# Where ScalarE copies a score maximum: ahead of both score pairs, or between them

## The reference

```
q, k, v = heads(ln(x) @ wq), heads(ln(y) @ wk), heads(ln(y) @ wv)   # 16 heads of 32
a = softmax(q @ k.T / sqrt(32))     # over the keys: 512 in a1, 1024 in a2
if causal: a = a * (key > query)    # masked after the softmax
o = a @ v
x_out = x + o @ li1 + b1
return x_out + gelu(ln(x_out) @ li2 + b2) @ li3 + b3
```

## Time and profile before

| | |
|---|---|
| median of 3 runs | 1487.85 us (1482.93 to 1493.84) |
| the profiled execution's own time | 1473.39 us |
| its span, first to last instruction | 1471.6 us |
| PE busy | 1408.9 us, 96% |
| DVE busy | 860.0 us, 58% |
| ACT busy | 761.9 us, 52% |
| POOL busy | 583.0 us, 40% |
| a1's steps | from about 797 to 914 us of the span |
| a2's steps | from about 1034 to 1246 us |

### The profile page before, as it was taken

One profiled execution on the slowest core, in us unless ns is written; L12 is line 12 of the kernel. 1 busy time (PEld: TensorE's weight loads), 2 busy tenths in 40 slices (PEclk: granted clock), 3 DMA queues, 4 the chain that ended last, 5 costly groups with the idle time before them and its releaser, 6 DMA issues.

```text
span 1471.6 us, 24770 instructions
## 1 busy us (share of the span) xinstructions
PE 1408.9 (96%) x9882; PEld 804.9 (55%) x9902; DVE 860.0 (58%) x1768; ACT 761.9 (52%) x1161; POOL 583.0 (40%) x657
## 2 busy tenths in 40 slices
PE   8999999999999989999899999999999999999997
PEld 5677853333333257885643334743344444768996
DVE  3288647669999555136854784346788882323221
ACT  4644225666666646333255776332687886333331
POOL 3053134232424332621113665401688887406111
PEclk9999999999999999999999999997799999998999
DMA  7000000000120039774000001403000000652100
GB/s 228 1 1 1 1 12 1 12 9 19 44 41 19 3 123 317 231 254 43 2 22 1 2 1 59 129 0 136 1 1 2 2 2 30 252 199 89 55 10 10
DMA packets 75210, 86.96 MB, mean 59 GB/s; under 512 B 27161, under 2 KB 60917, under 8 KB 73942
## 3 DMA queue, kind: packets, MB, share of 16 engines
q1 hardware_dynamic: 72182, 79.10, 17.0%
q0 software_dynamic: 2912, 6.26, 1.2%
HBM read 64.25 MB, written 21.37 MB: 58 GB/s over the span
## 4 chain that ended last, share of the span: by engine, by line
PE 80%; DVE 11%; POOL 3%; issue 2%; ACT 2%; DMA 1%; SPq 0%; POOLq 0%; DVEq 0%; ACTq 0%
PE psum L1715 11%; PE psum L1734 9%; PE psum L1679 6%; PE psum L4126 5%; PE psum L736 4%; PE psum L3387 4%; PE psum L3378 4%; PE psum L1931 4%; PE psum L1757 3%; DVE a_nm L1844 3%; PE psum L4137 3%; PE psum L3356 2%; PE psum L724 2%; PE psum L751 2%; PE psum L1965 2%
## 5 line engine op out<-in xcount | busy, mean ns | idle before, releaser
L1844 DVE TENSOR_REDUCE a_nm<-psum 128x1 f32<-128x512 f32 x302 | 198.4, 681 | 90.7 <-PE psum L1679 86.0
L1844 DVE TENSOR_REDUCE xa_nm<-psum 128x1 f32<-128x512 f32 x256 | 161.8, 682 | 49.6 <-PE psum L1679 44.1
L1769 ACT ACTIVATE xn<-psum 128x1024 f32<-128x1024 f32 (+1 forms) x96 | 86.2, 949 | 51.0 <-PE psum L1715 51.0
L1769 ACT ACTIVATE a_w<-psum 128x1024 f32<-128x1024 f32 x86 | 83.4, 1021 | 20.5 <-PE psum L1715 19.7
L1769 ACT ACTIVATE xa_w<-psum 128x1024 f32<-128x1024 f32 (+2 forms) x96 | 79.7, 885 | 19.6 <-PE psum L1715 19.4
L1715 PE MATMUL psum<-a2qT,a2kT 32*128 32x512 f32 x512 | 87.2, 608 | 0.0
L1679 PE MATMUL psum<-a2kr,a2qr 32*128 32x512 bf16 x256 | 73.2, 410 | 8.4 <-DVE a_nm L1844 7.1
L1679 PE MATMUL psum<-xa_ckr,xa_cqr 32*128 32x512 bf16 x256 | 65.8, 383 | 1.7 <-POOL xa_ckr L1978 1.0
L1679 PEld LDWEIGHTS psum<-a2kr,a2qr 32*128 32x128 bf16 x256 | 20.9, 92 | 83.3 <-DVE a_nm L1844 55.2
L1776 ACT ACTIVATE a_kept<-psum 128x512 f32<-128x512 f32 x82 | 49.3, 601 | 27.1 <-PE psum L1679 26.1
L1711 PE MATMUL psum<-a_mrow,onesb 3*128 3x512 bf16 x384 | 62.0, 390 | 0.2 <-ACT ctxT L1769 0.2
(11 more groups left out here) (590 smaller groups left out, 3487.8 us busy)
## 6 DMA issues: line engine op xcount, KB each, us to landing
mo_w<-in_L_ffn_W SPq DMA_DIRECT2D x14, 1024.0 KB, 7.4
sw_wv<-in_L_ffn_w_v SPq DMA_DIRECT2D x4, 2048.0 KB, 19.1
scratch_a2v<-co_stages SPq DMA_DIRECT2D x16, 256.0 KB, 3.4
scratch_a2k<-co_stages SPq DMA_DIRECT2D x16, 256.0 KB, 5.3
a2kT<-scratch_a2k SPq DMA_DIRECT2D x8, 512.0 KB, 8.2
a2v<-scratch_a2v SPq DMA_DIRECT2D x4, 1024.0 KB, 11.2
sw_wp<-in_L_ffn_w_proj SPq DMA_DIRECT2D x4, 1024.0 KB, 19.9
scratch_yd<-zero SPq DMA_DIRECT2D x8, 256.0 KB, 2.2
```

What stands on the lines that cost most here:

```text
L1769: e.activation(self.weights(n, c)[:, 2 * jj:2 * jj + 2, lo:S], ps[:, pr:pr + 2, lo:S], ACT.Exp, scale=self.scale).then_inc(*self.weighed.m ...
L1844: e.tensor_reduce(self.nm[n % 3][:, q, part, h:h + 1], view, AX.X, ALU.max, negate=True).then_inc(*self.max_taken.mark(*i))
```

## The change

In both attentions the kept maximum moves from ahead of the scores to between the two pairs, and the maximum ahead of the scores is a placed one, which DVE reads from its bank. The planner's condition is gone. The number of maxima per step, the two behind the scores, the instructions themselves and all transfers stay.

```
     def pair_kept(self, n):
         if self.fits(n, "rows"):
+            yield from self.place(self.chosen((2, 3)))
+
+    def between_scores(self, n):
+        if self.a.kept and self.fits(n, "rows"):
             yield from self.keep(self.chosen((2, 3)))
-        if self.fits(n, "rows") and self.free() <= self.could("rows", [3]) + self.slack:
-            yield from self.place(self.chosen((2, 3)))
-            yield from self.held_taken()
-
-    def between_scores(self, n):
-        if self.held:
-            if self.fits(n, "rows"):
-                yield from self.place(self.chosen((2, 3)))
             yield from self.held_taken()
```

## The result

The changed kernel takes 1630.64 us, median of 6 runs (1620.85 to 1642.24). The kernel before, beside it, takes 1489.01 us, median of 6 (1482.93 to 1493.84). The ratio is 1.096 [1.092, 1.099], slower by 141.6 us. The forecast was 1659 (1582 to 1758), with 114 us for the loop (the longer step at an unchanged clock) and 57 for the clock. The profiles put the loop at 114 to 117 us and the clock at 22 to 26.

A forecast was written before the change was run, and what follows sets the result against it. PE's queue was taken as the bound, waiting for the late copy's bank. Profiled 1473.4 us + 114 for the loop + 57 for the clock gave 1644; with the 14.5 median offset 1659 us, range 1582 to 1758.

The forecast's parts named there:

- What bounds the kernel: In a1 and a2 PE's queue is the bound, busy 25.57 of 25.94 us in a job of a2.
- rival D: The change moves little, as the planner already places the maximum so or skips the kept one: 1488 us, chance 0.03.
- The copy on ACT, and the fourth maximum behind it: In each step, t being the placed maximum's start: copy starts t+2.3 behind exponential 0, fourth maximum not before t+2.95.
- The placed maximum ahead: On PE, one maximum ahead of the scores, the other between the pairs, both covered by score 0: 0 us.
- The sum of the loop: At unchanged clock, +82 us over a2's 55 steps and +32 over a1's 27, together +114 us.
- The clock: PE's pauses put 22 of 82 steps at the lower clock, +2.6 us each: +57 us, bounded by 0 and +213.
- rival B: The clock is down nearly throughout a1 and a2, in 70 of 82 steps: 1784 us, chance 0.12.
- The offset: The median of the runs shown, 1487.85 us, lies 14.5 above the profiled execution; added to the forecast.
- A: The wait in a1 and a2 comes, but no step beyond the present ones at clock 0.50: 1602 us, chance 0.32.
- C: Not slower: the copy fits in a gap and the fourth maximum doesn't wait: 1466 us, chance 0.03.

The follow-up runs named there:

- a1_only: The change made in a1 alone, with a2 left as in the kernel before: 1533.28 us, ratio 1.032.
- copy_second: The kernel before with its copy moved behind exponential 0 on ACT alone, PE's order unchanged: 1657.24 us, ratio 1.118.
- copy_first: The changed kernel with the copy put back ahead of exponential 0 on ACT, PE's order as changed: 1537.25 us, ratio 1.035.
- padded: The changed kernel with four zero-weight matmuls in PE's pause ahead of the fourth maximum, in most steps: 1608.94 us, ratio 1.083.
- two_copies: The changed kernel with each copy made twice, the second one read: 1749.94 us against 1461.72 before, ratio 1.196.

## Why the forecast was right, and which term was not

**What bounds the kernel**: right. PE's queue was nearly full and stayed the bound; a1_only leaves a2 alone. The stretch between a1's last copy and a2's first is 141.7 us for 142.5, and the differences ahead of a1 and behind a2 are there in other kernels too. One reading was a little off: seven jobs of a2 have 56 steps, not 55 (rival D).

**The copy on ACT, and the fourth maximum behind it**: right in every time of the step. Forecast t+2.3 and t+2.95, measured t+2.28 and t+2.93. The releaser is the copy, as named, 143.0 us on DVE and 90.5 on PE (100 and more were forecast for PE; 128.7 if PE's weight loads are asked). copy_second shows that ACT's order alone does it. copy_first shows that undoing it alone takes nearly two thirds of the loss away (ratio 1.096 to 1.035).

**The placed maximum ahead, "costs nothing by itself"**: right for the change as made, not by itself. The other half, the kept maximum between the pairs, costs 0.49 us a step with ACT's order repaired. I took it to be covered by score 0, because its row starts beside it; its signal isn't. In the sum it is hidden behind exponential 0, so no number was wrong.

**The sum of the loop**: right. Counted as in the forecast, from jobs at full clock, it is 114 us: (37.82 - 25.94) / 8 x 55 = 82 in a2, and (19.21 - 14.49) / 4 x 27 = 32 in a1. Padded has 117, 36.4 in a1 and 80.3 in a2; its a1 isn't back at a clock of 1.00 (0.95, with three steps touched), which accounts for most of the excess there. A step at full clock is 4.67 us (4.68 forecast). PE is busy for 28.27 of the 37.82 us, 75%, where I had said about 68%.

**The clock**: 57 forecast, 22 to 26 measured, the one mis-sized term. Padded gives 22. What the two stages grew by in the profiles, 45.6 + 93.5 = 139.1 us, less the 114 of the loop leaves some 26. The count of steps held: 22 of 82 are touched by the lower clock in the trace, 11 in a1 and 11 in a2 (3 in a2 in the kernel before). That it fits is in part luck, as I had laid the 22 to four fifths of a1's steps, or spread them over a1 and a2's start, and a2's steps behind its start have seven of the touched ones. The price didn't hold: I gave each step 2.6 us, as if it were at 0.50 from end to end, and it came to 1.0 to 1.4 (22 us over 22 steps, 26 over the 19 more than before). Rows of a2's start show its parts to be right for such steps (ACT at the lower clock: exponential 0 of one step; PE: score 0's first row and the values with their next maximum):

```profile
1109.37 1.94 PE L1730 MATMUL psum<-xnT,a2v 128*32 128x512 f32 x8
1111.24 0.60 PE L1675 MATMUL psum<-a2kr,a2qr 32*128 32x512 bf16 x1
1111.24 0.61 PE L1707 MATMUL psum<-a_mrow,onesb 3*128 3x512 bf16 x2
```

```profile
1113.60 1.02 ACT L1765 ACTIVATE a_w<-psum 128x1024 f32<-128x1024 f32 x1 [3.90 <-PE psum L1711]
```

1.87 from values to next maximum and 2.36 from score to exponential, the figures of the earlier trace rows. But seven of a2's eleven touched steps look like this one, PE later in a2:

```profile
1244.89 1.93 PE L1730 MATMUL psum<-a_w,a2v 128*32 128x512 f32 x8
1246.58 1.09 PE L1753 MATMUL psum<-xnT,ones 128*32 128x256 f32 x8
...
1251.19 1.07 PE L1730 MATMUL psum<-a_w,a2v 128*32 128x512 f32 x8
```

Values and denominators are slow, and the next step's values run at full clock again. The step is 6.31 us for 4.67, +1.64. The nearest row that I had, 37 us at 0.50 in the lead-in the earlier trace rows, showed a clock that stays down. In a2's later steps it came back within the step. At a2's start it did not: PEclk is 0.50 from 1100 to 1118 us, though PE works there for some 5 us between two pauses (1108.84 to 1114.00). In a1 it was down for parts of up to three steps in a row. So that a step has 3 us of work without a pause, my argument against rival B, does not alone explain when the clock returns, and no run here does. The forecast had 31 to 35 us too much for the clock, and the loop was right or 3 us short.

**The offset** of 14.5 us for the profiled execution: right in the medians (1489.01 beside the changed kernel, for 1487.85). In the profiles it lies ahead of a1 and behind a2. 1489.0 + 114 + 26 = 1629, against 1630.6. The six runs of the changed kernel also differ by their clock: 1620.85 us at a mean of 0.965, 1642.24 at 0.950.

**The rivals.** A (the clock stays, 1602) is nearly what padded shows, 1608.94. The changed kernel itself lies midway between A and the forecast. B (1784) did not occur at this pause, but two_copies comes near its mechanism, with a pause of 2.08 us. The rule of the Trainium skill's page "TensorE: Matmul & The Clock Gate", section "A second HAM failure mode: psum-queue depth-cycling", which I weighed in the prediction, is borne out: PE pauses at its turn for a PSUM bank and the clock swings between both levels, now and then at pauses of 0.6 to 1.6 us (PEclk 0.92 in a2), in step after step at 2.08 (0.74). By it alone I would have leaned towards B, which is too far for this change. C and D are out: DVE waits for 82 of 82 copies, and the copy starts behind exponential 0 in the steps that I read.

## What to carry to other kernels

A bank handed back by an engine's copy is handed back when that engine's queue gets to the copy, so put such a copy ahead of anything in its queue that waits for work issued later. Cost a late hand-back from starts: here release, load, next block gave the step to 0.01 us. For the clock, price the part of a step that a fall of the clock covers and not the whole step (here 1.64 us for most of a2's, not 2.6), and measure it apart with pads of zero weights in the pause, which leave the loop as it is.

## What the runs showed of the hardware

- A matmul's signal to another engine came 1.16 us after its start instead of 0.42 when a group of float32 products was issued ahead of it on other rows, with its own semaphore too. The row's own duration (0.38 us) doesn't show it.
- Four zero matmuls in most pauses made the kernel faster by 20 us (ratio 1.083 for 1.096) at an unchanged step of 4.67 us, by the granted clock alone. Seven took about 100 us from the kernel with the longer pause (1.127 for 1.196), with PEclk in a2 at 0.94 for 0.74.
- With a pause of 2.08 us in a step of 6.9, a2's granted clock was 0.74; with one of 0.6 to 1.6 in 4.7 it was 0.92. PE was busy for 71% and 76% of the two stretches, so my comparison with stretches of 65 and 69% at 1.00 was a weak one.
